# Audio tower, token experts of the last stage: the second layer with its matrix as weights, gates spread through DRAM, gate weights made behind the ranking

## What is computed

```python
logits = einsum('bsh,he->bse', x, gate_w) + gate_b        # x = layernorm(h), 8 experts
topk_vals, topk_idx = top_k(logits, 2)
topk_weights = softmax(topk_vals, axis=-1)
weights = einsum('bske,bsk->bse', one_hot(topk_idx, 8), topk_weights)
hid = relu(einsum('bsh,ehf->bsef', x, w1) + b1)           # 128 -> 256
expert_out = einsum('bsef,efh->bseh', hid, w2) + b2       # 256 -> 128
h = h + einsum('bseh,bse->bsh', expert_out, weights)
```

## Time and profile before

| what | value |
|---|---|
| median of three runs | 2226.64 us |
| profiled execution: its time | 2225.99 us |
| profiled execution: its span | 2223.8 us |
| TensorE busy | 2017.7 us, 91% |
| VectorE busy | 1574.1 us, 71% |
| ScalarE busy | 1070.4 us, 48% |
| GpSimd busy | 646.2 us, 29% |
| first hidden matmul of the tail | at 1510.82 us |
| mean granted clock of TensorE | 0.97 |

### The profile page before, as it was taken

How to read it: one execution, slowest core, us unless ns; L and a number is a source line. 1 busy time by engine, 2 the same in 40 slices (tenths; PEclk the granted TensorE clock), 3 DMA queues, 4 the chain that set the end, 5 groups by cost and what they waited for, 6 DMA issues and landing times. The chain is left out here.

```text
span 2223.8 us, 55170 instructions
## 1 busy us (share of the span) xinstructions
PE 2017.7 (91%) x21100; PEld 1795.5 (81%) x21100; DVE 1574.1 (71%) x4080; ACT 1070.4 (48%) x2699; POOL 646.2 (29%) x856
## 2 busy tenths in 40 slices
PE   8599999989647999987999999999999999999998
PEld 6497777778535888876777777789999999999998
DVE  5746556554584765665999999977777777777774
ACT  4433333332344565653677777744444344444443
POOL 0202222210015555521444444442122212221220
PEclk9899999999877999998999999999999999999999
DMA  8100011000211111100000000000000000000000
GB/s 189 45 1 12 13 14 13 12 6 1 78 54 40 44 37 40 39 19 1 3 3 3 4 3 4 3 2 1 15 7 7 7 14 7 7 7 14 7 8 15
DMA packets 80549, 44.54 MB, mean 20 GB/s; under 512 B 45864, under 2 KB 74088, under 8 KB 80008
## 3 DMA queue, kind: packets, MB, share of 16 engines
q1 hardware_dynamic: 73416, 29.26, 5.9%
q0 software_dynamic: 5888, 12.07, 2.0%
q10 hardware_dynamic: 1024, 0.26, 0.1%
HBM read 27.20 MB, written 14.38 MB: 19 GB/s over the span
## 5 line engine op out<-in xcount | busy, mean ns | idle before, releaser
L2146 ACT ACTIVATE w<-banks,b 128x384 f32<-128x384 f32 (+1 forms) x512 | 259.6, 572 | 393.6 <-PE banks L2221 393.5
L2203 PE MATMUL banks<-w,w 128*128 128x128 f32 (+1 forms) x3072 | 364.1, 275 | 0.0
L2203 PEld LDWEIGHTS banks<-w,w 128*128 128x128 f32 (+1 forms) x3072 | 350.4, 189 | 9.1 <-issue 8.7
L1699 POOL TENSOR_TENSOR t<-eb 128x256 f32<-128x256 f32 (+1 forms) x288 | 199.6, 726 | 248.2 <-ACT eb L1674 210.2
L1729 PE MATMUL banks<-qT,w 64*64 64x128 f32 (+1 forms) x4608 | 265.9, 268 | 4.2 <-ACT eb L1674 2.4
L1737 PE MATMUL banks<-eb,w 64*64 64x128 f32 (+1 forms) x4608 | 268.9, 270 | 0.5 <-DVE eb L1628 0.3
L1729 PEld LDWEIGHTS banks<-qT,w 64*64 64x64 f32 x4608 | 245.7, 133 | 21.1 <-issue 13.8
L1737 PEld LDWEIGHTS banks<-eb,w 64*64 64x64 f32 x4608 | 244.1, 133 | 1.3 <-DVE eb L1628 1.1
L2043 DVE SCALAR_TENSOR_TENSOR h<-banks,t_wt,h 128x128 f32 (+3 forms) x672 | 183.6, 341 | 82.5 <-PE banks L2203 79.1
L1252 POOL DMA_INDIRECT xg<-xs,rowu x184 | 181.0, 984 | 129.1 <-DMA xg<-xs,rowu 86.8
L1628 DVE TENSOR_TENSOR eb<-eb,rd 128x1536 f32<-128x1536 f32 x96 | 191.9, 1999 | 9.4 <-ACT rd L1685 8.1
(11 more groups left out here) (307 smaller groups left out, 4281.5 us busy)
## 6 DMA issues: line engine op xcount, KB each, us to landing
out<-h SPq DMA_DIRECT2D x16, 320.0 KB
xs<-r_xl SPq DMA_DIRECT2D x16, 192.0 KB, 2.7
xg<-xs,rowu POOLq DMA_INDIRECT x184, 2.5
h<-in_xT SPq DMA_DIRECT2D x3, 750.0 KB, 14.4
h<-in_xT SPq DMA_DIRECT2D x3, 749.0 KB, 17.4
xs<-r_xl SPq DMA_DIRECT2D x16, 128.0 KB
blocks<-NT SPq DMA_DIRECT2D x24, 48.0 KB, 1.9
D<-blocks SPq DMA_DIRECT2D x24, 48.0 KB, 2.0
```

The source lines that it names most:

```text
L1699: nc.gpsimd.tensor_tensor(t1[:, n % 2, 0:m, 2 * s:2 * s + 2].rearrange("p t v -> p v t"), e[:, v:v + 2, 0:m], e[:, v + 2:v + 4, 0:m], ALU. ...
L2146: nc.scalar.activation(gb[u % 2][:, f, s * GW:s * GW + NFREE[s]], k.ps[:, order.bank(n), 0:NFREE[s]], ACT.Relu, bias=k.b1_1[:, 2 * e + f:2 ...
L2203: last = nc.tensor.matmul(k.psf[0:n, o:o + P], gb[u % 2][:, f, c * P:c * P + n], k.w2_1[:, 2 * e + f, :], start=(f == 0), stop=(f == 1))
```

## The change

1. **Second layer.** The second matrix becomes the stationary operand and `gb` moves, in two parts of 384 and 362 tokens. The output now has the features on partitions and the tokens along the row.
2. **Gates.** A gate weight per token then belongs along the row, the same on all 128 partitions. `wT` (48 rows, chunk and expert, by 128 tokens) is stored to DRAM (`k.gates`, double), and SP loads for each expert its six rows, broadcast to all partitions, into `wtb` (two buffers, 384 KB each). Expert n's load waits until VectorE has used the one before last.
3. **Sum.** `gated` multiplies output and gates (two products, from PSUM into `parts`, which lies in the room of `k.video`), and adds them into `sums` (two sums, SBUF); expert 0 writes `sums` directly. New pieces `back`, two at expert 2 of the next sequence, turn `sums` back, and `returned` adds them to h. The store of the result moves behind that, on SP's queue behind the load for expert 5.
4. **Order.** `weigh` comes right behind `rank`; the exponential comes behind the hidden pieces of expert 7, `wT` at expert 0 behind `turn_o`, `logits` into the midst of expert 7's hidden pieces, `turn_x` as a whole to expert 6. Expert 7 is the last of one sequence, expert 0 the first of the next.
5. Smaller things: the tokens' sum goes into h in place (the tile `t_hx` is gone), `xT` has two buffers instead of four, the first pair is written out ahead of the loop on TensorE and VectorE, and `room` asks the banks at the start of a pair a little more strictly.

```diff
             par, e = divmod(u, E1)
             front = not (last_pair and par)
-            out += [("hidden", x, u) for x in range(4)]
+            out += [("hidden", x, u) for x in range(2)]
+            if e == 7 and front:
+                out.append(("logits", 0, u))
+            out += [("hidden", x, u) for x in range(2, 4)]
             if e == 0 and front:
                 out += [("turn_o", g, u) for g in range(2)]
+            if e == 0:
+                out.append(("wT", 0, u))
             if e == 1 and front:
                 out += [("lin", g, u) for g in range(2)]
             if e == 2:
-                out.append(("wT", 0, u))
+                out += [("back", g, u) for g in range(2)]
             if e == 3:
                 out += [("bias", g, u) for g in range(2)]
-            if e in (5, 6) and front:
-                out.append(("turn_x", e - 5, u))
-            if e == 7 and front:
-                out.append(("logits", 0, u))
+            if e == 6 and front:
...
-                for b in range(B):
-                    sp.wait_ge(added, E1 * (b + 1) + 2)
+
+                def store(b):
+                    i, par = divmod(b + 1, 2)
+                    if i < PAIRS:
+                        last_pair = i == PAIRS - 1
+                        sp.wait_ge(freed, order.emptied(i, order.find("back", 1, par, last_pair), True, last_pair))
+                    else:
+                        sp.wait_ge(freed, order.emptied(PAIRS - 1, len(order.ending) - 1, True, True) + 2)
                     sp.dma_start(k.out[b, 0:T - LAST, :].rearrange("(c p) d -> p c d", p=P),
                                  k.h[:, b, 0:NC - 1, :]).then_inc(k.stored, 16)
                     sp.dma_start(k.out[b, T - LAST:T, :], k.h[0:LAST, b, NC - 1, :]).then_inc(k.stored, 16)
+
+                for b in range(B):
+                    i, par = divmod(b, 2)
+                    last_pair = i == PAIRS - 1
+                    gates = k.gates[b % 2]
+                    sp.wait_ge(free, order.emptied(i, order.find("wT", 0, par, last_pair), False, last_pair))
+                    sp.dma_start(gates, wT[:]).then_inc(gates_out, 16)
+                    sp.wait_ge(gates_out, 16 * (b + 2))
+                    for e in range(E1):
+                        n = b * E1 + e
+                        if n >= 2:
+                            sp.wait_ge(added, n + 1)
+                        row = gates.rearrange("(c e) t -> e c t", e=E1)[e]
+                        sp.dma_start(wtb[:, n % 2], row.partition_broadcast(P)).then_inc(gates_in[n % 2], 16)
+                        if e == 5 and b:
+                            store(b - 1)
+                store(B - 1)
                 sp.wait_ge(k.stored, 32 * B)
 
             @block.vector
...
                     par, e = divmod(u, E1)
                     dve.wait_ge(o_ps, i * U + (u + 3))
+                    dve.wait_ge(gates_in[u % 2], i * (8 * U) + 16 * (u // 2 + 1))
                     if e:
-                        dve.wait_ge(added, i * U + (u + 2))
-                    if e == 2:
-                        dve.wait_ge(freed, order.emptied(i, order.find("bias", 1, par, last_pair), True, last_pair))
-                    for c in range(NC):
-                        n = rows(c)
-                        o = 2048 + (u % 2) * 1024 + c * P
-                        hh = k.h[0:n, seq(i, par), c, :]
-                        last = nc.vector.scalar_tensor_tensor(out=hh, in0=k.psf[0:n, o:o + P],
-                                                              scalar=wt[0:n, par, c * E1 + e:c * E1 + e + 1],
-                                                              in1=hh if e else hx[0:n, c, :], op0=ALU.mult, op1=ALU.add)
+                        dve.wait_ge(folded, i * (2 * MORE) + (par * MORE + e))
+                    acc = sums[:, par]
+                    gate = wtb[:, u % 2].rearrange("p c t -> p (c t)")
+                    for s in range(2):
+                        at = slice(s * GW, s * GW + NFREE[s])
+                        last = nc.vector.tensor_tensor(parts[:, at] if e else acc[:, at],
+                                                       k.ps[:, 4 + u % 2 * 2 + s, 0:NFREE[s]], gate[:, at], ALU.mult)
                     last.then_inc(added, 1)
-
-                def body(i, last_pair):
+                    if e:
+                        dve.wait_ge(added, i * U + (u + 3))
+                        for s in range(2):
+                            at = slice(s * GW, s * GW + NFREE[s])
+                            last = nc.vector.tensor_tensor(acc[:, at], acc[:, at], parts[:, at], ALU.add)
+                        last.then_inc(folded, 1)
+
+                def returned(b, i, n, last_pair, biased):
+                    dve.wait_ge(freed, biased)
+                    bank = group(k.ps[:, order.bank(n), 0:GW])
+                    dve.wait_ge(full, order.filled(i, n))
+                    hh = k.h[:, b, 0:GC, :]
+                    nc.vector.tensor_tensor(hh, hh, bank, ALU.add).then_inc(freed, 1)
+                    bank = group(k.ps[:, order.bank(n + 1), 0:GW])
+                    dve.wait_ge(full, order.filled(i, n + 1))
+                    hh = k.h[:, b, GC:NC - 1, :]
+                    nc.vector.tensor_tensor(hh, hh, bank[:, 0:GC - 1, :], ALU.add)
+                    hh = k.h[0:LAST, b, NC - 1, :]
+                    nc.vector.tensor_tensor(hh, hh, bank[0:LAST, GC - 1, :], ALU.add).then_inc(freed, 1)
+
+                def back(i, par, last_pair, first):
+                    n = order.find("back", 0, par, last_pair)
+                    if first and par == 0:
+                        for g in range(2):
+                            dve.wait_ge(full, order.filled(i, n + g))
+                            nc.vector.memset(blank[:, g:g + 1], 0.0).then_inc(freed, 1)
+                    elif par:
+                        returned(seq(i, 0), i, n, last_pair,
+                                 order.emptied(i, order.find("bias", 1, 0, last_pair), True, last_pair))
+                    else:
+                        returned(seq(i, -1), i, n, last_pair, order.emptied(i, -1, True) - 1)
+
+                def body(i, last_pair, first):
                     for u in range(U):
...
                         front = not (last_pair and par)
-                        if e == 1:
-                            weigh(i, par)
-                            if front:
-                                linear_sum(i, par + 1)
+                        if e == 1 and front:
+                            linear_sum(i, par + 1)
+                        if e == 2:
+                            back(i, par, last_pair, first)
                         if e == 2 and front:
...
                             rank(i, par + 1)
+                            weigh(i, par + 1)
                         if u:
                             gated(i, u - 1, last_pair)
                     gated(i, U - 1, last_pair)
...
                         par, e = divmod(u, E1)
                         act.wait_ge(full, order.filled(i, n))
+                        if kind == "wT":
+                            act.wait_ge(gates_out, i * 32 + (par * 16 + 16))
...
-                        if x == 3 and e == 0:
-                            act.wait_ge(ranked, nth(i, par, RANKS, RANKED))
-                            nc.scalar.activation(mx[:, 0, :], pm[:], ACT.Exp).then_inc(expd, 1)
-
+                        if x == 3 and e == E1 - 1 and not (last_pair and par):
+                            exponent(i, par + 1)
+
+                def exponent(i, q):
+                    act.wait_ge(ranked, nth(i, q, RANKS, RANKED))
+                    nc.scalar.activation(mx[:, 0, :], pm[:], ACT.Exp).then_inc(expd, 1)
...
                         empty(0, 0, kind, x, n % 4)
...
-                        pe.wait_ge(freed, order.emptied(i, -1, True) - (n < 3))
+                        pe.wait_ge(freed, order.emptied(i, -1, True) - (n < 1))
 
...
+                        w = NFREE[s]
+                        for f in range(2):
+                            last = nc.tensor.matmul(k.ps[:, 4 + u % 2 * 2 + s, 0:w], k.w2_1[:, 2 * e + f, :],
+                                                    gb[u % 2][:, f, s * GW:s * GW + w], start=(f == 0), stop=(f == 1))
+                    last.then_inc(o_ps, 1)
+
+                def turn_back(par, x, bank):
+                    acc = sums[:, par]
+                    for j in range(GC):
+                        c = x * GC + j
                         n = rows(c)
-                        o = 2048 + (u % 2) * 1024 + c * P
-                        for f in range(2):
-                            last = nc.tensor.matmul(k.psf[0:n, o:o + P], gb[u % 2][:, f, c * P:c * P + n],
-                                                    k.w2_1[:, 2 * e + f, :], start=(f == 0), stop=(f == 1))
-                    last.then_inc(o_ps, 1)
-
-                def body(i, last_pair):
```

(29 more changed lines are left out.)

37 lines of the change are left out of this document (26 added, 11 removed).

## The result

The changed kernel takes 2262.25 us (median of 4 runs, 2257.89 to 2267.33) against 2227.95 us for the kernel before in the same session: ratio 1.0156, 95% interval 1.0142 to 1.0170. It is slower, in the predicted range (2240 to 2308) and 18 us under the forecast: the kernel grew by 34 us, where I had 53. The profiled execution took 2257.89 us. First its page: span, busy times, and the new groups of the second layer.

The account below looks back on a forecast made before the run. A loop across VectorE and TensorE was to replace TensorE as the tail's bound, 47.5 us against 44.4: +45.6 on the 2223.8 us span gave 2269.4, 2272 as median, plus 8 for the clock: 2280 us, range 2240 to 2308.

Parts of the forecast that it names:

- the collisions: In gated 1 and gated 4, SBUF sums slowed by GpSimd: 2.3 us a sequence, bounds 0 and 4.
- a period that is neither 45 nor 47 to 48: Sign of a wrong prediction: the tail's time per sequence, in us, matching neither the loop without nor with GpSimd collisions.
- L2081 waiting for the load: Sign of a wrong prediction, pointing to (b): VectorE's gated product waits for the load of its gates.
- TensorE's terms: TensorE's count in the tail: 0.16 us less an expert, turns +0.66, 0.57 wait gone; 43.2 us a sequence.
- VectorE's part: From VectorE's first add of the returned sum to the gate weights: 34.0 us, plus 2.3 for collisions.
- TensorE's part: From the turn of the gate weights (wT) to the next returned sum: 11.2 us, taken for every loop.
- the way through DRAM: Storing and loading the gates: 8.2 us (to 10), hidden since gated 0 is due 8.8 us behind wT; costed at nothing.
- the clock: TensorE's idle time ahead of L2257 lowers its clock two or three times in fourteen loops, 3.2 us each: +8.
- The ends: Outside the loops: +2.0 us at the tail's start, +2.5 behind the last output, -0.6 in the last sequence.
- (a): Rival: the loop without collisions, 45.2 us a sequence, so 2240 us; 16%.
- (c): Rival: TensorE's own count decides, where the loop is below 44.24 us; 2213 us, faster; 7%.
- (b): Rival: the gates come late, or the clock falls in most loops; 2300 to 2330 us; 13%.

Follow-up runs that it names:

- pool_short: The changed kernel with GpSimd's second-half scaling cut to 4 of 128 columns and token splits to 16 of 384; 2251.17 us, ratio 1.0073.
- two_straight_long: The changed kernel with ranking ahead of norm_out, 3 KB gate rows, VectorE's program without loop or branch, two gate buffers; 2233.28 us, ratio 0.9993.
- order_only: The kernel before with only the change's new order, keeping the old second layer, per-token gates and adds to h; 2227.44 us, ratio 1.0007.
- long_rows: The changed kernel with weights ordered expert, chunk, so gate loads are 128 pieces of 3 KB, not 768 of 512 B; 2260.63 us, ratio 1.0119.
- four_straight: first_four with VectorE's program written out for all pairs, without a loop and its branch; 2234.23 us, ratio 0.9998.
- rank_first: The changed kernel with norm_out moved right behind the gate weights and its turns to the middle of expert 1; 2283.34 us, ratio 1.0252.
- first_four: As rank_first, with four buffers for the spread gates instead of two; 2252.14 us, ratio 1.0128 to the kernel before.
- first_long: rank_first, with two gate buffers and the loop's branch, plus the 3 KB gate rows of long_rows; 2243.63 us, ratio 1.0049.

## Why the prediction was right, step by step

What held is the mechanism: the loop over both engines decides, with the collisions inside. Its size was too large, and the time alone would not have told the forecast from its rival without collisions: 2262 lies 18 us under the one and 22 over the other. The loops did not settle it either. My sign of being wrong was "a period that is neither 45 nor 47 to 48", and they take 46.5 and 45.9 us; "L2081 waiting for the load" was another, and it waits. It is the long rows of L2088, and pool_short, that tell the two apart.

**TensorE's terms** held within 0.6 us a sequence. A plain expert is 1817.63 - 1813.07 = 4.56 us, as forecast (my working of the output's 2.51 us adds up to 2.48). With the loop out of the way a sequence took 43.8 us against the 43.2 predicted; two_straight_long shows some 0.2 of that as waits for norm_out's turns. The rest I can't place; the 0.57 us that I counted as saved did not come back in order_only either.

**VectorE's part** was forecast at 36.3 us and measured at 35.3 and 35.5. Two thirds of the difference are the collisions: 2.3 in the sum, 0.82 + 0.81 = 1.6 in the rows, because GpSimd's operation starts a little behind the first sum and the second waits for only part of it. Pool_short measured 1.6 and 1.3 a loop for them. The last third is open. **TensorE's part** was 11.2 us in one kind of loop, as forecast.

**The steps that were mis-sized** are two: VectorE's part, above, in every loop, and "TensorE's part, from wT to the next returned sum: 0.11, output 2.51, hidden 2.06 ...", taken for every loop. At the start of a pair the output of expert 7 stands ahead of the turn of the weights, not behind it: the body of a pair ends with it. TensorE then needs 8.6 us to L2292, and the gates decide, with 10.4 us. Loops of 46.5 and 45.9 us, 46.2 in the mean, stand against the 47.5 forecast. For 14 loops that is 14 x 1.3 = 18 us too many: VectorE's part was on average 0.9 us too long, which makes some 12 of them, and TensorE's 0.4, some 6.

**"I cost at nothing" the way through DRAM** was wrong on half the loops. The load took 6.5 us, past my bound of 6, since its 768 pieces are of 512 B; the 4.2 us of the earlier trace rows was for long ones. Gated 0 waits in 15 sequences. It costs 1 us where TensorE's part is short (long_rows), none where it is long.

**The sum.** The 15 periods came to +28.8 us, for which I had 43.7 - 0.8 - 1.2 = 41.7 and 8 for the clock. One period is not like for like: the last grew from 42.29 to 44.07 us, where I had 1.2 less, since before, with the turn at expert 2, it already lacked the front's turns and linear pieces. The clock fell in one loop of fourteen, not in two or three: that loop took 48.15 us, 1.7 more than its like, where I had 3.2. TensorE's stop ahead of L2257 is 2.03 us at the end of one loop and 0.35 at the end of the next; I had put up to 2.3 us in every loop, and 3 to 5 us of idle time a sequence where the windows have 2.1. The ends, forecast at 2.0 + 2.5 - 0.6 = 3.9, came to 34.6 - 28.8 = 5.8: the last turns wait 2.45 us for gated 7, whose gates came 0.70 late. The parts ahead of the tail ran 2.7 us earlier in this execution than in the one of before; the change does not touch them.

**The rivals.** (a), no collisions, and (c), TensorE's count, both needed another kernel: pool_short is (a), and ran at 44.6 to 44.9 us a loop; two_straight_long is (c), with 3.4 us off the tail where (c) had 14: 0.6 us a loop make 8 to 9 of the difference, the ends the rest. The bound given for (c) was wrong: 44.24 us is the loop at which the kernel would be no slower than before; TensorE's own count decides only below its 43.2, which needs VectorE's part 2.0 us shorter, not 1.0. Of (b), late gates, half was true, at a small price. Its reason, that nobody reads one line of DRAM 128 times, was wrong: the broadcast in the earlier trace rows does. That the loop is the cause is shown from both sides, by times and tails: with the order and no returned sums nothing is lost (order_only), and with the sums, and 5.2 us of VectorE's work moved out of VectorE's part, nothing is lost either, once the two waits behind it, for the gates and at the branch, are gone (four_straight).

## What to carry to other kernels

When a result of one engine is fed back a stage later, add up the whole loop across the engines, for each place in a loop body apart: the first unit of a body may have another neighbour than the others. Look at the queue between the value fed back and the value waited for; work that nobody in the loop needs (norm_out here) belongs on its other side. And count DMA loads by their pieces: the same bytes in 3 KB rows landed in 3.5 us, in 512 B rows in 6.5.

## What the runs showed of the hardware

- A loop's branch on VectorE costs 2.0 to 2.3 us at the start of a pair with no loads ahead of it, 2.3 to 3.1 in long_rows, 4.7 to 5.0 in rank_first with two gate loads just issued, and 5.8 to 6.6 in first_four with up to four: with more gate loads under way the page of instructions, one packet on q14, comes later, or (long_rows) takes 0.9 to 1.7 us itself, where it took 0.5 to 0.8 in the changed kernel. In first_long it is 2.9 to 3.3. In the kernel before, VectorE stood 1.58 us at this place, put down to ScalarE's exponential, which had ended 0.7 us earlier; TensorE, which decided there, did not wait for it. Timelines of VectorE and ScalarE before:

```profile
1782.30 0.17 DVE L2015 TENSOR_SCALAR t_pm<-t_mx 128x6 f32<-128x6 f32 x1 [1.58 <-ACT t_mx L2150]
...
1781.40 0.20 ACT L2150 ACTIVATE t_mx<-t_pm 128x6 f32<-128x6 f32 x1
```

- A load of 384 KB to all partitions took 6.5 us in 512 B pieces from rows 4 KB apart, 3.5 us in 3 KB pieces, and 10.8 us in 512 B pieces from rows 8 KB apart in an input tensor. Whether the spacing or the tensor's place does the last wasn't tried.
- A sum of two SBUF tiles beside a GpSimd operation takes 0.8 us longer (1.82 for 1.00 a pair), and the GpSimd operation 0.2 (1.20 for 1.00); products from PSUM were never longer in these traces than 0.56 us each.
